# First attention of a four-layer kernel: who divides the turned outputs by their sums

## The reference

```python
qkv = x @ W_qkv
q, k, v = jnp.split(qkv, 3, axis=-1)          # then split into 16 heads
scores = jnp.einsum('bhnd,bhmd->bhnm', q, k) / jnp.sqrt(jnp.float32(D_MODEL))
attn = jax.nn.softmax(scores, axis=-1)
out = jnp.einsum('bhnm,bhmd->bhnd', attn, v)
out = out.transpose(0, 2, 1, 3).reshape(B, N, D_MODEL)
```

## Time and profile before

| | |
|---|---|
| median of 3 runs | 1024.18 us (1024.17 to 1026.49) |
| the profiled execution | 1023.77 us |
| its span, first to last instruction | 1021.7 us |
| TensorE busy | 979.9 us (96%) |
| VectorE busy | 826.8 us (81%) |
| ScalarE busy | 732.8 us (72%) |
| GpSimd busy | 523.6 us (51%) |
| mean granted TensorE clock | 0.999 of full speed |

### The profile page before, as it was taken

The page is one execution under the profiler, slowest core; times in us unless marked ns, Lnnn a source line. Parts: engine busy times, 40 slices in busy tenths (PEclk is TensorE's granted clock), DMA queues, the critical chain, the costliest instruction groups (busy, mean ns, idle before and its releaser), DMA issues. The chain is left out here.

```text
span 1021.7 us, 20122 instructions
## 1 busy us (share of the span) xinstructions
PE 979.9 (96%) x5769; PEld 469.4 (46%) x5769; DVE 826.8 (81%) x1811; ACT 732.8 (72%) x945; POOL 523.6 (51%) x631
## 2 busy tenths in 40 slices
PE   8999999999999999999999999999999999999996
PEld 4422222222222246888888887863232333222585
DVE  7999999999999867889788789987666666644677
ACT  4377887878888776655555555668889888999753
POOL 3051744726538745677677676675443144310275
PEclk9999999999999999999999999999999999999999
DMA  7661223122130005323433432443422332230011
GB/s 229 205 226 48 81 64 109 45 87 95 40 109 17 3 4 165 122 87 127 143 99 95 154 115 80 151 147 98 150 87 68 92 123 73 66 108 1 1 32 52
DMA packets 73548, 97.04 MB, mean 95 GB/s; under 512 B 12620, under 2 KB 42188, under 8 KB 73100
## 3 DMA queue, kind: packets, MB, share of 16 engines
q1 hardware_dynamic: 73496, 96.40, 29.7%
HBM read 68.18 MB, written 27.79 MB: 94 GB/s over the span
## 5 line engine op out<-in xcount | busy, mean ns | idle before, releaser
L780 DVE TENSOR_REDUCE a_nmax<-a_ps_f 128x1 f32<-128x512 f32 x512 | 319.7, 683 | 7.7 <-PE a_ps_f L627 5.3
L542 ACT ACTIVATE a_prob<-a_ps_s 128x1024 f32<-128x1024 f32 x256 | 250.0, 1022 | 63.5 <-PE a_ps_s L683 62.3
L1428 ACT ACTIVATE a_prob<-a_ps_s 128x1024 f32<-128x1024 f32 x256 | 244.4, 1026 | 27.8 <-PE a_ps_s L1480 26.8
L2248 POOL TENSOR_TENSOR moe_hl<-moe_hid,moe_hh 128x512 fp32r<-128x512 f32 x134 | 174.2, 1305 | 84.1 <-ACT moe_hh L2129 84.0
L627 PE MATMUL a_ps_f<-a_ks,a_qs 48*128 48x512 bf16 x512 | 156.9, 384 | 10.7 <-DVE a_nmax L780 3.1
L2119 ACT ACTIVATE moe_ps<-moe_ps 128x512 f32<-128x512 f32 x128 | 74.5, 582 | 111.6 <-PE moe_ps L2042 110.8
L1493 PE MATMUL a_ps_o<-a_prob,a_va 128*32 128x512 f32 x1024 | 136.4, 605 | 1.8 <-DVE a_turned_o L1608 1.2
L696 PE MATMUL a_ps_o<-a_prob,a_va 128*32 128x512 f32 x1024 | 136.4, 605 | 0.5 <-ACT a_prob L542 0.4
L683 PE MATMUL a_ps_s<-a_qs,a_ks 51*128 51x512 bf16 x512 | 131.8, 381 | 1.7 <-ACT a_prob L542 1.4
L627 PEld LDWEIGHTS a_ps_f<-a_ks,a_qs 48*128 48x128 bf16 x512 | 38.5, 93 | 193.9 <-DVE a_nmax L780 188.1
L2170 DVE TENSOR_TENSOR moe_prod<-moe_cw,moe_ps 128x512 f32<-128x512 f32 x128 | 87.3, 682 | 27.4 <-PE moe_ps L2042 26.7
(11 more groups left out here) (324 smaller groups left out, 1636.1 us busy)
## 6 DMA issues: line engine op xcount, KB each, us to landing
moe_cw<-r_weights SPq DMA_DIRECT2D x256, 128.0 KB, 2.8
parts_q<-a_parts SPq DMA_DIRECT2D x48, 256.0 KB, 2.5
parts_k<-a_parts SPq DMA_DIRECT2D x48, 256.0 KB, 2.6
a_qs<-parts_q SPq DMA_DIRECT2D x126, 96.0 KB, 2.4
a_ks<-parts_k SPq DMA_DIRECT2D x126, 96.0 KB, 2.4
out_x<-g_X SPq DMA_DIRECT2D x7, 256.0 KB, 2.3
a_prob<-in_x_t SPq DMA_DIRECT2D x3, 512.0 KB, 5.4
moe_wg<-in_wg SPq DMA_DIRECT2D x1, 1088.0 KB, 6.7
```

Of the source, the lines that this page charges most:

```text
L542: nc.scalar.activation(prob[:, u % PSLOTS, :, :], ps_s[:, u % 2, :, :], ACT.Exp, scale=float(P) ** -0.5).then_inc(exp_done, 1)
L780: nc.vector.tensor_reduce(nmax[:, half_no, h % 2, col:col + 1], ps_f[:, bank, :], AX.X, ALU.max, negate=True).then_inc(max_done, 1)
L1428: nc.scalar.activation(prob[:, u % PSLOTS, :, :], ps_s[:, u % 2, :, :], ACT.Sigmoid, scale=float(HD) ** -0.5).then_inc(exp_done, 1)
L2248: nc.gpsimd.tensor_tensor(hl[:, part_at(j), :], hid[:, hid_at(j), :], hh[:, part_at(j), :], ALU.subtract).then_inc(hl_done, 1)
```

## The change

For all outputs but the second of batch 6 and the two of batch 7 the division is cut into three parts on three engines. ScalarE copies the whole turned tile (128x512) from its PSUM bank to a new SBUF tile `turned_o` (`take_turned`), in its own stream at o0 and o1, and counts that in a new semaphore `o_copied`; TensorE's next user of the bank waits for that count and no longer for `att_done`. VectorE takes the reciprocal from `turned_o` at turn 50 (for o0) and at turn 13 (for o1), four turns later each (`REC_AT`, `invert`). GpSimd does the two multiplies (its own `divide`): the first half's behind the `split_max` of half 0, the second half's between the `split_max` of half 1 and `add_x`. ScalarE and the reciprocal wait until the multiplies of the output before are done, since there is one `turned_o` and one `rec`.

```diff
+REC_AT = (50, 13)
+        turned_o = sb("turned_o", [P, T])
+        o_copied = sem("o_copied")
...
+            def take_turned(b, n):
+                act.wait_ge(att_done, NO * b + n + ATT_C)
+                take(turned_o[:, :], ps_f[:, BANK[f"o{n}"], :], ot_done, NO * b + n + 1 + OT_C, o_copied)
...
+                            if back and t == "o0" and not is_last(b):
+                                take_turned(b, 0)
+                            if tail and t == "o1" and not is_last(b):
+                                take_turned(b - 1, 1)
...
-                    pe.wait_ge(att_done, NO * (b - 1) + (int(t[1]) + 1) % NO + ATT_C)
+                    count = NO * (b - 1) + (int(t[1]) + 1) % NO
+                    if is_last(b - 1):
+                        pe.wait_ge(att_done, count + ATT_C)
+                    else:
+                        pe.wait_ge(o_copied, count)
...
+            def invert(b, n):
+                dve.wait_ge(o_copied, NO * b + n + 1)
+                dve.wait_ge(att_done, NO * b + n + ATT_C)
+                nc.vector.reciprocal(rec[:, :, :, :], output_parts(turned_o[:, :])[:, :, :, :, HD]).then_inc(rec_done, 1)
...
-                            if back and t == "o0":
+                            if back and t == "o0" and is_last(b):
                                 divide(b, 0)
-                            if tail and t == "o1":
+                            if tail and t == "o1" and is_last(b):
                                 divide(b - 1, 1)
+                            if back and t == REC_AT[0] and not is_last(b):
+                                invert(b, 0)
+                            if tail and t == REC_AT[1] and not is_last(b):
+                                invert(b - 1, 1)
...
+            def divide(b, n):
+                o, to = output_parts(turned_o[:, :]), outputs_of(att, n)
+                pool.wait_ge(rec_done, NO * b + n + 1)
+                for q in range(PER_O):
+                    ins = nc.gpsimd.tensor_tensor(to[:, :, :, q, :], o[:, :, :, q, 0:HD],
+                                                  rec[:, :, :, q].unsqueeze(3).broadcast_to([P, NT, HG, HD]), ALU.mult)
+                ins.then_inc(att_done, 1)
...
                 if u0 == 0 and tail:
+                    if not is_last(b):
+                        divide(b - 1, 1)
                     add_x(b - 1)
...
+                    if back:
+                        divide(b, 0)
```

## The result

The changed kernel takes 1053.82 us, the kernel before 1024.30 us: a ratio of 1.0283 with an interval of 1.0254 to 1.0313. It is slower, by 29.5 us; forecast were 23.6 us and 1047.8 us, with a range that ends at 1056. The profiled execution took 1052.85 us with a span of 1051.0, 29.3 us over the span of before.

A forecast was written before the change was run, and what follows sets the result against it. VectorE was the engine to follow, its divisions filling gaps TensorE leaves, with GpSimd's chain 0.05 us from late. 1024.2 + 20.35 (batches 1 to 5) + 2.95 (batch 6) + 0.30 (batch 0) gave 1047.8 us; range 1041 to 1056.

The forecast's parts named there:

- The bound: VectorE at o0 and o1: the division fills a gap TensorE leaves, so removing its 0.79 us is worth nothing.
- faster: Rival at o1 and o0: TensorE's chain moves up with VectorE, each moved division gives 0.49 us, 1017.8 us; chance 0.06.
- ScalarE's copy: ScalarE at o0 and o1: one more 128x512 pass of 0.60 us, fits its gaps, costed at nothing.
- The reciprocal: VectorE at turns 13 and 50: 0.30 us each, covered by nothing, 13 times, 3.9 us.
- The multiplies: GpSimd ahead of its sum: two multiplies of 0.46 us, 0.92 us in all, and 0.08 us between dependent steps.
- The late sum: GpSimd's sum starts 3.77 us later, delaying the split of half 0: 4.07 us per batch 1 to 5, 2.95 in batch 6.
- reciprocals only: Rival: splits not late for TensorE, divisions still in gaps, only 3.9 us of reciprocals remain, 1028.1 us; chance 0.08.
- The weight splits: GpSimd after batch 6's multiplies: three weight splits start later, using up 4.33 us of idle time; 0, at most 1 us.
- The clock: TensorE in the stalls: granted clock stays at 1.00; the rival, that it falls, adds 7 us, 1055 us; chance 0.18.

The follow-up runs named there:

- no_division: Kernel before without the divisions of the first seven and a half batches, a one-column copy on VectorE in each place: 1023.93 us, ratio 1.0004.
- splits_first: Changed kernel; in batches 1 to 5 GpSimd makes its splits before the sum and the normalisation: 1029.13 us, ratio 1.0056.
- warm_in_stall: Changed kernel with 14 useless TensorE matmuls ahead of the transpose of max0 in batches 1 to 6: 1045.75 us, ratio 1.0207.
- pool_dose: Kernel before, division still on VectorE, with one useless GpSimd power operation ahead of each sum of batches 1 to 6: 1048.72 us, ratio 1.0244.
- rec_in_gaps: Changed kernel with the reciprocals at turns 47 and 11 in place of 50 and 13: 1037.61 us, ratio 1.0115.
- gaps_mt_copy_first: Changed kernel, GpSimd's splits first, reciprocals at turns 11 and 47, maxima's transposes at 12 and 48, ScalarE's copy of them before an exponential: 1025.39 us, ratio 1.0019.

## Why the prediction was right, point by point

**The bound.** That removing the division is worth nothing held: 0.79 us of wait ahead of maximum 11 against 0.8 forecast, and no_division takes the time of before. The rival *faster*, which lived on VectorE's fullness, needed the sum early; in splits_first_gaps GpSimd's splits are on time in batches 1 to 5 and it still isn't faster, so this rival fails at its first step (TensorE's chain doesn't move up with VectorE), not only at its condition.

**ScalarE's copy.** In the changed kernel it cost nothing, as forecast: 0.60 us at 123.70, in ScalarE's idle time and under the stall. Without the stall it isn't quite free at o0, since its cover was counted for ScalarE alone and score 47 waits for the bank: 0.2 us in batch 1 of splits_first.

**The reciprocal** took a slot of 0.26 us (102.50 to 102.76) where 0.30 was taken; 13 times that is 3.4 in place of 3.9 us.

**The multiplies** took 0.79 us a pair where 0.92 was taken from the sum of two tensors in the earlier trace rows. The step from them to the sum took 0.18 us where 0.08 was taken, so the two sizes nearly cancel. The Trainium skill's figure (GPSIMD Engine Reference, section 3.1), an estimate of 0.28 us each, is below the 0.39 us measured; the nearest row was the better guide.

**The late sum.** It started 4.64 us after turn 8 (4.83 forecast), which is 3.58 us late (3.77). A batch of warm_in_stall, where the clock stays up, lost 4.25 us of stall and 0.79 us of wait at o1, plus two reciprocals (0.52), less two divisions (1.58): 3.98 us, where 4.07 was forecast. Batch 6 of the changed kernel, with its 3.26 us of stall, lost by the same count 2.99 us (2.95). With the measured sizes the forecast's own sum is 5 x (3.58 + 0.26) + (3.58 - 1.12 + 0.26) + 0.26 = 22.2 us; warm_in_stall has 22.2 us, or 21.7 without what its matmuls overrun. That it fits so well is in part luck. From one maximum 47 to the next a batch of warm_in_stall takes 45.3 us (128.18 to 173.44) and before 41.7 (123.83 to 165.53, for maximum 46), 3.6 us more; the count by rows, 3.98, is some 0.4 too high. And 0.7 of the 22.2 us come behind this stage, where the forecast had nothing. pool_dose shows the same chain without the change. The rival *reciprocals only* is out by the stalls themselves. The weight splits, counted as 0 and at most 1 us, make the last split of half 1 late and cost 0.3 us (3.17 us of wait ahead of VectorE's first copy of the next part, 2.84 before).

**The clock** is the step that was wrong, by the prediction's own sign ("or if the clock falls there"), though the time lies in the range. The forecast took the granted clock to stay at 1.00 and gave the fall a chance of 0.18, on the ground that the one fall seen before came after a longer idle time. The falls came in five of six stalls, at 3.4 us of TensorE's idle time, and in rec_in_gaps at 1.4 us. One fall behind one idle time said only that such a time is enough, not that a shorter one isn't. The price was sized well, as a rival: 7 us, against 7.1 us between the spans. The Trainium skill (TensorE: Matmul & The Clock Gate, section on why this matters for your kernels) warns of idle stretches between bursts of matmuls. The runs agree with the warning: in the profiles the clock fell behind 17 of 18 idle times of 1.4 to 3.4 us that nothing filled, also behind those of 1.4 us, which are shorter than the ones it warns of. The forecast's own bounds ended at 1053 us; the median of 1053.82 us lies next to that rival's 1055, and in the range because the range had been reached out to it. So the number came out by a mechanism to which the prediction gave 0.18, on top of the one to which it gave 0.68. Without the clock's term, at 1045.75 us, the forecast of 1047.8 us is 2 us too high.

## What to carry to other kernels

Before work moves from a full engine to one that looks half idle, look at what ends the waits on both: here the full engine's work lay in a gap that TensorE leaves, while GpSimd, at work 51% of the span, carried in this stage an in-order chain with 0.05 us of slack. Put what another engine waits for first in the order of such a chain, and what nobody needs soon behind it; that alone gave back 25 of 29 us, the falls of the clock among them. And charge each new idle stretch of TensorE twice, once for its length and once for the slower matmuls behind it.

## What the runs showed of the hardware

The granted clock fell from 1.00 to 0.50 (2.4 to 1.2 GHz) behind idle times of TensorE of 3.4 us (batches 1 to 5 of the changed kernel), 2.6 us (the same batches of pool_dose) and 1.4 us (those of rec_in_gaps), and was near 1.00 again 3.5 to 8 us later. Filling the idle time with 14 matmuls of no use, 3.2 us, kept it up in every batch. What decides in which of the stalls it falls stays open: in batch 6 it didn't behind 2.43 us of TensorE's idle time in the changed kernel, but did behind 2.26 us in splits_first and 1.60 us in pool_dose. Nor does it take such a stall: the fall of 55 to 65 us in the profile of gaps_mt_copy_first came while no wait of TensorE was longer than 0.4 us (40 to 70 us). GpSimd's power function took 3.07 us for 17 elements in each partition, 0.18 us an element.
